# Building the stacked score operand of a vector quantizer: the high parts by transfers instead of ScalarE copies

## What is computed

```python
x = x + _L0_conv_ref(_gn(x), ...)        # group norm, Haar split, convolutions, attention, inverse Haar
x = x + _L1_conv_ref(_gn(x), codebook)   # group norm, then each pixel is replaced by its nearest code

def _L1_conv_ref(x, codebook):           # codebook: 512 codes of 32 channels
    xf = x.reshape(b * h * w, d)
    dists = x_sq - 2.0 * (xf @ codebook.T) + c_sq
    idx = jnp.argmin(dists, axis=1)
    return codebook[idx].reshape(b, h, w, d)
```

## Time and profile before

| | us |
|---|---|
| median of 3 runs | 2288.87 |
| lowest and highest run | 2281.72, 2294.78 |
| span of the profiled execution, first to last instruction | 2164.4 |
| what lies around the span, by the median of the runs (2288.87 - 2164.4) | 124.5 |

### The profile page before, as it was taken

How to read it: one execution, slowest core, us unless ns; L and a number is a source line. 1 busy time by engine, 2 the same in 40 slices (tenths; PEclk the granted TensorE clock), 3 DMA queues, 4 the chain that set the end, 5 groups by cost and what they waited for, 6 DMA issues and landing times. The chain is left out here.

```text
span 2164.4 us, 27115 instructions
## 1 busy us (share of the span) xinstructions
PE 1984.8 (92%) x5232; PEld 946.5 (44%) x5232; DVE 1810.3 (84%) x3979; ACT 1059.2 (49%) x2018; POOL 1252.3 (58%) x1299
## 2 busy tenths in 40 slices
PE   6999999999999999999999999999999999995653
PEld 3444455444544455444544445444544445442221
DVE  4122799988999799988999899988999889888996
ACT  5134645545555545546556454546455454543331
POOL 2001277654776377663776367673776457673876
PEclk9999999999999999999999999999999999995555
DMA  6000011111110112111111111111111011110111
GB/s 203 15 10 5 20 40 43 27 29 34 46 35 21 41 36 47 25 24 41 42 36 26 42 35 41 30 24 37 43 41 26 20 25 34 30 25 20 34 37 32
DMA packets 80459, 76.97 MB, mean 36 GB/s; under 512 B 29200, under 2 KB 62608, under 8 KB 80016
## 3 DMA queue, kind: packets, MB, share of 16 engines
q1 hardware_dynamic: 45776, 50.78, 8.3%
q0 software_dynamic: 32768, 16.84, 5.2%
q10 hardware_dynamic: 1728, 7.41, 0.9%
HBM read 41.36 MB, written 16.78 MB: 27 GB/s over the span
## 5 line engine op out<-in xcount | busy, mean ns | idle before, releaser
L1053 POOL DMA_INDIRECT vqc<-in_codebook,idx x1024 | 1000.9, 977 | 545.2 <-DVE idx L964 306.4
L542 PE MATMUL ring<-hf,w_sb 128*128 128x512 f32 x1824 | 888.5, 600 | 2.9 <-ACT hf L715 2.9
L487 PE MATMUL score<-cst,yst 98*128 98x512 f32 x1024 | 788.4, 777 | 83.8 <-DVE idx L964 54.8
L960 DVE MAX8 top<-score 128x8 f32<-128x512 f32 x1024 | 695.3, 684 | 74.7 <-PE score L487 63.8
L964 DVE FIND_INDEX8 idx<-top,score 128x8 uint32<-128x512 f32 x1024 | 704.2, 690 | 0.0
L666 ACT CAST yst<-bands 32x256 fp32r<-32x256 f32 x1024 | 411.3, 402 | 174.6 <-PE score L487 162.1
L542 PEld LDWEIGHTS ring<-hf,w_sb 128*128 128x128 f32 x1824 | 341.6, 191 | 316.9 <-issue 294.2
L487 PEld LDWEIGHTS score<-cst,yst 98*128 98x128 f32 x1024 | 204.0, 202 | 395.0 <-DVE idx L964 206.3
L542 PE MATMUL ring<-ha,w_sb 128*128 128x512 f32 x704 | 347.5, 598 | 5.1 <-DVE ha L853 4.6
L542 PE MATMUL ring<-hb,w_sb 128*128 128x512 f32 x544 | 262.6, 595 | 6.8 <-DVE hb L866 6.8
L627 ACT ACTIVATE z<-ring,prm 128x512 f32<-128x512 f32 x144 | 99.0, 688 | 273.3 <-PE ring L542 272.7
(11 more groups left out here) (101 smaller groups left out, 1276.8 us busy)
## 6 DMA issues: line engine op xcount, KB each, us to landing
xnat<-in_x SPq DMA_DIRECT2D x128, 128.0 KB, 2.7
yst<-yl SPq DMA_DIRECT2D x512, 32.0 KB
vqc<-in_codebook,idx POOLq DMA_INDIRECT x1024
out<-vqc SPq DMA_DIRECT2D x128, 128.0 KB
w_sb<-in_weights ACTq DMA_DIRECT2D x1, 1920.0 KB, 8.2
w_sb<-in_weights ACTq DMA_DIRECT2D x3, 384.0 KB, 12.8
w_sb<-in_weights ACTq DMA_DIRECT2D x1, 1152.0 KB, 15.6
w_sb<-in_weights ACTq DMA_DIRECT2D x1, 960.0 KB, 8.6
```

The lines of the kernel that those rows point to most:

```text
L487: nc.tensor.matmul(score[BANK["tile", t]][:, :], yst[0:KST, j % 2, g, wp], cst[0:KST, :], start=True, stop=True).then_inc(s_tile, 1)
L542: t = nc.tensor.matmul(ring[g % RING][:, :, :], w_sb[:, SLOTS[n, m, kind, ky], :], own(source(n, m, kind), half, slice(PAD + di, PAD + di ...
L960: nc.vector.max(top8[:, t % 4, :], score[BANK["tile", t]][:, :]).then_inc(s_top, 1)
L1053: nc.gpsimd.indirect_dma_start(vqc[:, c % 2, w * CH:(w + 1) * CH], None, codebook[:, :], bass.IndirectOffsetOnAxis(idx[:, c % 2, k, 0:1], ...
```

## The change

`stack_high` is removed with its semaphore, and with it all 8 ScalarE casts of a block. `yh`, which already holds the same high parts as a tile, is the source in its place: `stack` now issues 12 transfers for each block, four from `yh` to part 0, four from `yh` to part 2 and then the four from `yl` to part 1, all behind the one wait for `yl`. TensorE waits for all 12 on one semaphore. Because the transfers now read `yh`, `high` may overwrite it only when the transfers of the block two before have landed; before it waited for `yl`.

```diff
@@
-STACKED = 16 * BLK
+STACKED = 16 * BLK * PARTS
@@ def stack(v, j):
                 sp.wait_ge(s_yl, JN * v + j + 1)
-                for g in range(BLK):
-                    sp.dma_start(yst[CH:2 * CH, j % 2, g].bitcast(F32),
-                                 yl[g * CH:(g + 1) * CH, j % 2].bitcast(F32)).then_inc(s_yst[j % 2], 16)
+                for part, src in ((0, yh), (2, yh), (1, yl)):
+                    for g in range(BLK):
+                        sp.dma_start(yst[part * CH:(part + 1) * CH, j % 2, g].bitcast(F32),
+                                     src[g * CH:(g + 1) * CH, j % 2].bitcast(F32)).then_inc(s_yst[j % 2], 16)
@@ def tile(v, t):
             if t % JTILES == 0:
-                    pe.wait_ge(s_ysth, 2 * (JN * v + j + 1))
                     pe.wait_ge(s_yst[j % 2], STACKED * ((JN // 2) * v + j // 2 + 1))
@@ def high(v, par, j):
                 act.wait_ge(s_band, v + 1)
                 if j >= 2:
-                    act.wait_ge(s_yl, JN * v + j - 1)
+                    act.wait_ge(s_yst[j % 2], STACKED * ((JN // 2) * v + j // 2))
                 nc.scalar.copy(yh[:, j % 2], block_of(par, j)).then_inc(s_yh, 1)
-
-            def stack_high(v, par, j, part):
-
-                if j >= 2:
-                    act.wait_ge(s_tile, TILES * v + JTILES * (j - 1))
-                for g in range(BLK):
-                    t = nc.scalar.copy(yst[part * CH:(part + 1) * CH, j % 2, g],
-                                       block_of(par, j, slice(g * CH, (g + 1) * CH)))
-                t.then_inc(s_ysth, 1)
@@ ScalarE's body
                         for j in range(2):
                             high(v, 1 - par, j)
-                        for part in (0, 2):
-                            stack_high(v, 1 - par, 0, part)
                     elif quant and what == "tile":
                         j, k = step[1] // JTILES, step[1] % JTILES
-                        if k in (1, 3) and j + 1 < JN:
-                            stack_high(v, 1 - par, j + 1, k - 1)
                         if k == JTILES // 2 and j + 2 < JN:
                             high(v, 1 - par, j + 2)
```

More of the change, by code:

```diff
@@ L329, in conv_vq_kernel @@
         s_yl = sem("s_yl")
-        s_ysth = sem("s_ysth")
         s_yst = [sem(f"s_yst{i}") for i in range(2)]
```

## The result

The changed kernel took **2345.9 us** (median of 4 runs, 2341.33 to 2350.3) against 2288.52 us (4 runs, 2281.72 to 2294.78) of the kernel before on the same chip: ratio 1.0241, 95% interval 1.0212 to 1.027. It is slower by 57 us. The forecast was 2298 us in a range from 2284 to 2316, so the time lies outside it.

The account below looks back on a forecast made before the run. PE, 92% busy, was taken as the bound. Terms 14.3 + 1.9 + 2 + 1.6 - 9.7 - 1.4 = +8.7 us, put on the runs' median of 2288.87, gave 2298 us, range 2284 to 2316.

Parts of the forecast that it names:

- its whole time isn't given; the 124.5 us around the span are untouched, so I put the sum on the median: Added +8.7 us to the runs' median of 2288.87 us, though the profiled execution's span was 2164.4 us.
- What it costs is how late the last of twelve lands: Transfers behind the wait for `yl`: eight more issues at 0.62 us each delay each block's first tile.
- Rival 1: SyncE's issues slow down in a burst of twelve or 24, making blocks late: 2404 us; chance 0.05.
- 9.0 us from `yl` to the first tile: Every block: 4.1 us with four transfers plus 8 x 0.62 us for the eight added issues.
- Stalls at the image starts, +14.3 us: Block 0 of seven images: the tile came 6.7 to 7.4 us after `yl`, so PE stalls 1.6 to 2.3 us each.
- Relief of `ync`, -9.7 us: Image starts: without the casts `ycopy` comes 3.3 us sooner, ending PE's 11.8 us of waits in 8 cases, less usual pauses.
- Relief of `br`, -1.4 us: PE's weight loads waiting for ScalarE's `br`: casts gone, 0.2 us saved in each of seven images.
- Block 15, +2 us: Last block of the seven images: cover short by 0.5 to 0.9 us, 4.2 us in all, part swallowed by VectorE's backlog.
- the stall is swallowed: After image-start stalls PE resumes with VectorE caught up, winning back some 9 us of 14.3: 2289 us; chance 0.17.
- Last image, +1.9 us, GpSimd bound: Its start stalls 1.9 us; later tiles 5 us later cost nothing because gathers, 1.25 us apart, have slack.
- Clock, +1.6 us: New gaps of some 1.7 us in seven images may drop PE's clock, 1.6 us a fall; one fall taken.
- rival 3: The clock falls at every new stall, 11.2 instead of 1.6 us, and block 15 costs 4.2 us: 2309 us; chance 0.18.

Follow-up runs that it names:

- half and half: Against the kernel before: part 0 by four casts, part 2 by transfers, eight transfers a block; 2160.07 us, ratio 0.9964 (quick set), 2288.23 us, 1.0143 (slow set).
- the relief alone: Kernel before without casts; its four transfers a block take `yh` to part 0, other parts zero; 2159.82 and 2158.56 us, 0.997 and 0.9957, both quick sets.
- the one with more transfers: Kernel before, casts kept, eight more 30-partition transfers a block from `yh` to unread partitions, two waits added; 2166.24 us (quick set), 2390.01 us (slow set).

## Why the prediction was wrong, and where it was right

By its own steps:

- **"its whole time isn't given; the 124.5 us around the span are untouched, so I put the sum on the median"** is the step that failed. In every profiled execution span and time differ by about 2 us (2341.7 and 2343.53; 2165.1 and 2166.88). The span of 2164.4 and the median of 2288.87 were not one execution with 124.5 us around it, but two conditions in which the same kernel runs. Every price in the sum was read from a trace of the quick one, and the result was measured in the other. There the changed kernel costs 57 to 63 us, in the quick one about 4.
- **"What it costs is how late the last of twelve lands"** put everything else that a transfer could cost at nothing, and no rival had a price for each transfer. That fails in the slow sets: with the `yh` part issued early 39 us stay. Rival 1 came nearest (transfers cost more in a burst, 2404 us), but through slower issues, and the median issue stayed at 590 ns. Divided by the transfers added, the slow sets give half and half +30 us for 512, changed +57 and +63 us for 1024, i.e. about 0.06 us a transfer; with the early issues +39 us, 0.04; the kernels with two more waits and 30 partitions 0.12 to 0.13. The runs show that the engines stand still together more often and that the bytes hardly matter. By what path the edits do that, and why the same edit is free in a quick set, they don't show.
- **9.0 us from `yl` to the first tile**: right, 8.9 to 9.4 us at the start of every image in all four traces of the changed kernel, in either condition. Block 15 of the images with convolutions came at 9.0 to 9.2, and in the quick sets' last image nearly every block at 8.9 to 9.2.
- **Stalls at the image starts, +14.3 us**: 14.3 us in 6 cases by the weight loads' row; the intervals between neighbouring loads give 12.9 us beyond the usual. Right.
- **Relief of `ync`, -9.7 us**: right; by the same intervals 10.0 us in 7 cases, now none.
- **Relief of `br`, -1.4 us**: too small. The waits fell from 23.8 to 7.0 us, by intervals from 12.2 to 3.3 us, -8.9 us. One followed image isn't seven.
- **Block 15, +2 us, and the rival "the stall is swallowed"**: PE doesn't win the stall back. It waits 21 us more for VectorE's index at the weight loads (13.6 us by intervals, 29.6 before and 43.2 now), more than was put in for block 15. Not all of it comes from the stalls: with the relief alone, which has none, the same row is 99.4 us against 87.1. So over half of the growth, 12 us of 21, goes with the relief: PE waits for ScalarE less and for VectorE more.
- **Last image, +1.9 us, GpSimd bound**: right. It took 200.9 us instead of 198.9, and the gathers stand 1.25 us apart to the end:

```profile
2154.20 0.69 DVE L950 FIND_INDEX8 idx<-top,score 128x8 uint32<-128x512 f32 x1
...
2158.41 0.94 POOL L1039 DMA_INDIRECT vqc<-in_codebook,idx  x1 [0.30 <-issue]
...
2159.66 0.94 POOL L1039 DMA_INDIRECT vqc<-in_codebook,idx  x1 [0.31 <-issue]
```

- **`high`, put at nothing**: ScalarE waits for the transfers 94.0 us in 12 cases, 77 of them in the last image; nothing shows that it costs time.
- **Clock, +1.6 us**: not to be told in the quick sets, where the mean granted clock is 0.948 and 0.951 changed and 0.950 twice before. In the slow set it falls from 0.940 to 0.932, which rival 3 comes nearest to, though it had the falls at the image starts alone.
- **The sum, +8.7 us**: +4.3 and +3.5 us in the quick sets. The relief alone gave -6.9 and -8.6 there, so what was added cost some 11 to 12 us (the sum had 19.8 for it, and -11.1 for the relief). The sum was 4 to 5 us too high in the condition that it described, and says nothing about the other. That it came so near is in part luck: the terms as measured by intervals add up to 12.9 + 2.0 + 13.6 - 10.0 - 8.9 = +9.6 us, so `br`, 7.5 us too small, and VectorE's index, 11.6 us too small, nearly cancelled, and some 6 us between +9.6 and the measured +4 stay unexplained.
- **"A rule against the change"** drew no term of the sum. Its 2 us for a transfer is the figure that the Trainium skill (DMA: Bandwidth & Descriptors, "Anatomy of one DMA") gives for the path from GpSimd, while these transfers go out from SyncE.

The prediction named the signs by which it would be wrong: issues wider apart than 0.7 us, and holes between the gathers of the last image. In the trace of the result an issue begins 0.75 us or more behind the one before it in its block of twelve 79 times, 37 times in the changed kernel of a quick set; and in the last image gathers around tile 42 began 0.9 us after their index, where the quick set has 4.4 us, so that GpSimd was at times not the bound there.

## What to carry to other kernels

Before a sum is put on a median, hold the trace's own span against it: if they differ by more than the few us that lie around a span, trace and runs are of two conditions, and prices that the trace shows at zero aren't bounded from above by it. The same 1024 transfers were nearly free in one condition and went with 0.04 to 0.13 us each in the other, so among edits that are level, the one with fewer DMAs is the safer by these runs, whatever they carry. And moving work from an idle engine to a queue pays only for what the engine delayed (here 8 us of 411); if the queue's issues lie behind a wait, issue what doesn't need it first.

## What the runs showed of the hardware that wasn't expected

- **One kernel, two times on one chip.** 2167.12 and 2258.66 us for the same program on the same chip in two sets. In the slow sets rows name "remote", the kernels with added transfers have issues of 3 to 98 ns, and the trace holds fewer DMA semaphore records (11,730 in the kernel before against 28,671). Waits of the kernel before in a slow set:

```profile
PEld score L487 <- issue: 262.2, 740, 4.9
...
DVE top L960 <- remote: 34.1, 14, 4.1
```

  Whether the thin records are a sign of the cause or only go with it stays open; no run could choose its condition. A rival that the runs don't exclude is that recording slows the core, since a span stands on record for every execution of the quick and slow sets, so that none of them ran unrecorded. One form of it fails, a fixed price for each semaphore record: the changed kernel and the one with more transfers have nearly the same number in full traces (52,501 and 52,879), but a slow set takes 150 us more than a quick one for the first (2321.6 - 2171.1) and 224 us more for the second (2390.0 - 2166.2). Also open is what the casts cost in the slow condition.
- **The price there is hardly one of size**: +131 us for 1024 transfers of 30 KB and +125 us for 1024 of 1.9 KB. The Trainium skill (DMA: Bandwidth & Descriptors, "Rules for kernel authors") says to join small transfers because below 64 KB one pays mostly overhead. The slow sets agree with its direction, if the price is the transfers' and not that of the waits beside them, and by one that falls on every engine rather than on the one who waits; the quick sets don't show it (+1.4 us).
- **30 partitions cost more to issue than 32**: 779 ns in the median against 590, for 30 KB and for 1.9 KB alike. (They also go to partitions 98 to 127, where no transfer of 32 goes; no run tells the two apart.) The queue's packets are 48 a transfer with 32 partitions ((94,928 - 45,776) / 1024) and 45 with 30 ((91,856 - 45,776) / 1024), that is 16 or 15 besides one for each partition. The Trainium skill (DMA: Bandwidth & Descriptors, "Why a DMA increments its semaphore by 16 and not by 1") has such a transfer run on 15 of the 16 engines, with the issuing engine writing the missing increment itself; the packet counts agree.
- **The gathers' packets can take 14 times as long**: the same 32,768 packets took 655 ns in the mean instead of 47, and 59.7% of the DMA engines' time instead of 4.5%, when the high parts were constant. That the cause is few, repeated rows is argued above and not shown.
